# Subtracting the row maximum of the nine kept scores on GpSimd instead of VectorE, in a top-12 attention kernel

## The reference

```python
xn = layernorm(x)                                  # no scale, no shift
q, k, v = split_heads(xn @ Wqkv.T + bqkv)
q, k = layernorm(q) * gamma_q + beta_q, layernorm(k) * gamma_k + beta_k
aw = softmax(q @ k.T / sqrt(8))                    # 256 x 256 a head
kth = top_k(aw, 12)[-1]                            # the 12th largest of each row
aws = aw * (aw >= kth); aws /= aws.sum(-1) + 1e-8
o_s = aws @ v                                      # sparse part
o_l = softmax(q) @ (softmax(k).T @ v) / (z + 1e-6) # linear part
o = a * o_s + (1 - a) * o_l                        # a = sigmoid(alpha), one a head
y = x + o @ Wproj.T + bproj + (xn @ W[i] + b[i])   # i chosen once from the logits
```

## Time and profile before

| | before |
|---|---|
| median of 3 runs | 1330.32 us (1327.15 to 1330.66) |
| span of the profiled execution | 1331.1 us |
| VectorE busy | 95% of the span |
| ScalarE busy | 86% |
| GpSimd busy | 83% |
| TensorE busy (matmuls) | 78% |
| mean granted TensorE clock | 0.930 |

### The profile page before, as it was taken

One profiled execution on the slowest core, in us unless ns is written; L12 is line 12 of the kernel. 1 busy time (PEld: TensorE's weight loads), 2 busy tenths in 40 slices (PEclk: granted clock), 3 DMA queues, 4 the chain that ended last, 5 costly groups with the idle time before them and its releaser, 6 DMA issues.

```text
span 1331.1 us, 40027 instructions
## 1 busy us (share of the span) xinstructions
PE 1040.0 (78%) x8964; PEld 693.5 (52%) x8964; DVE 1260.1 (95%) x4916; ACT 1138.5 (86%) x3978; POOL 1110.9 (83%) x1458
## 2 busy tenths in 40 slices
PE   3787877778787878877888787777877788787776
PEld 1455555555455555555555455554555555555544
DVE  5799999999999999999999999999999999999995
ACT  3689998989899888989989899888989888898885
POOL 4588898979789888888879889798888888889874
PEclk9989999989899798998989989898998998989998
DMA  2222222112222122221112221112221212221210
GB/s 57 72 59 63 77 77 75 35 57 64 77 76 72 29 64 65 76 77 47 53 53 76 77 76 46 55 57 71 76 76 35 66 53 76 77 76 33 64 49 13
DMA packets 165131, 82.31 MB, mean 62 GB/s; under 512 B 7747, under 2 KB 164933, under 8 KB 164934
## 3 DMA queue, kind: packets, MB, share of 16 engines
q1 hardware_dynamic: 164934, 80.54, 20.9%
HBM read 42.77 MB, written 37.75 MB: 60 GB/s over the span
## 4 chain that ended last, share of the span: by engine, by line
DVE 57%; issue 33%; DVEq 6%; ACT 1%; POOL 1%; PE 1%; DMA 0%; SPq 0%; POOLq 0%
DVE rest L525 21%; DVE top L518 21%; DVE next L531 8%; DVEq L72 5%; DVE drop L615 2%; DVE o_sparse L574 1%; ACT e L719 1%; DVE den L566 1%; DVE k_sum L593 1%; DVE stats L582 0%; PE work_ps L910 0%; PE work_ps L911 0%; DVE x_mv L588 0%; DVE d_max L557 0%; DVE den L571 0%
## 5 line engine op out<-in xcount | busy, mean ns | idle before, releaser
L386 POOL TENSOR_SCALAR below<-e,next 128x256 bf16<-128x256 f32 x768 | 696.1, 922 | 21.5 <-DVE next L531 21.3
L719 ACT ACTIVATE e<-score_ps,drop 128x256 f32<-128x256 f32 x1024 | 472.4, 480 | 108.2 <-DVE drop L615 105.5
L838 PE MATMUL turn_ps<-ident,e 128*128 128x128 f32 x2048 | 429.9, 303 | 10.9 <-ACT kept L685 10.4
L525 DVE MATCH_REPLACE8 rest<-e 128x256 f32<-128x256 f32 x1024 | 413.3, 404 | 0.0
L531 DVE MAX8 next<-rest 128x8 f32<-128x256 f32 x1024 | 407.5, 408 | 0.0
L839 PE MATMUL turn_ps<-minus_huge,below 128*128 128x128 bf16 x2048 | 402.5, 232 | 0.0
L518 DVE MAX8 top<-score_ps 128x8 f32<-128x256 f32 x1024 | 359.4, 410 | 41.8 <-issue 21.7
L838 PEld LDWEIGHTS turn_ps<-ident,e 128*128 128x128 f32 x2048 | 312.2, 152 | 80.9 <-ACT kept L685 17.9
L685 ACT ACTIVATE kept<-turn_ps 128x512 f32<-128x512 f32 x512 | 285.1, 620 | 33.8 <-PE turn_ps L839 14.3
L839 PEld LDWEIGHTS turn_ps<-minus_huge,below 128*128 128x128 bf16 x2048 | 234.5, 115 | 0.0
L719 ACT ACTIVATION_READ_ACCUMULATOR e<-score_ps,drop 128x1 f32 x1024 | 217.1, 212 | 0.0
(11 more groups left out here) (141 smaller groups left out, 1540.6 us busy)
## 6 DMA issues: line engine op xcount, KB each, us to landing
part_slots<-part SPq DMA_DIRECT2D x128, 192.0 KB, 2.3
q_slots<-part_slots SPq DMA_DIRECT2D x64, 256.0 KB, 3.4
k_slots<-part_slots SPq DMA_DIRECT2D x64, 256.0 KB, 4.1
part_slots<-part SPq DMA_DIRECT2D x64, 128.0 KB, 1.9
x_sb<-in_L_attn_x SPq DMA_DIRECT2D x32, 128.0 KB, 3.6
x_res<-in_L_attn_x SPq DMA_DIRECT2D x32, 128.0 KB, 3.7
out_y<-out_sb SPq DMA_DIRECT2D x32, 128.0 KB, 4.2
w_ops<-in_L_ffn_W SPq DMA_DIRECT2D x1, 512.0 KB
```

What stands on the lines that cost most here:

```text
L386: nc.gpsimd.tensor_scalar(below[:, r, t, :], e[:, r, t, :], next8[:, r, t, TOPK - 9:TOPK - 8], None, ALU.is_lt).then_inc(s["below_pool"], 1)
L525: nc.vector.match_replace(rest[:, t, :], e8[:, (u_ - 1) % 2, t, :], e[:, (u_ - 1) % RING, t, :], REMOVED).then_inc(s["rest_ready"], 1)
L719: nc.scalar.activation(e[:, u_ % RING, t, :], score_ps[:, u_ % 2, t // 2, t % 2, :], ACT.Exp, bias=drop[:, u_ % 2, t, 0:1], accum_out=z[:, ...
L838: mm(dst, e[:, r, t, keys], ident[:], start=True, stop=False, is_transpose=True)
```

## The change

The subtraction leaves VectorE's slot. GpSimd does it, in each slot of an existing batch, behind its three comparisons and ahead of the work that followed those. It waits for the four searches of the unit (`top_ready`), and for the e8 of two units before (`e8_ready`), whose buffer it overwrites. VectorE now waits, before the first search of a unit, until the subtraction of two units before has read that buffer of `top` (`drop_ready`). A wait at GpSimd's set-up makes sure that the zeroes of `top` are written.

```diff
@@ gpsimd, set-up
             nc.gpsimd.memset(eps_row[:, :, D:VA], Z_EPS).then_inc(s["pool_const"], 1)
+            pool.wait_ge(s["pool_const"], 7)
@@ gpsimd, body, behind the three comparisons of a slot
+                    if exists(it):
+
+                        q = u_ % 2
+                        wait(pool, s["e8_ready"], g - 1)
+                        wait_alone(pool, s["top_ready"], TILES * (g + 1), s["waits_passed"])
+                        nc.gpsimd.tensor_tensor(drop[:, q], top[:, q], top[:, q, :, 1:2].to_broadcast(
+                            [P, TILES, 9]), ALU.subtract).then_inc(s["drop_ready"], 1)
                     if u_ == 1 and exists(it + 1):
                         normalise(it, 0)
@@ vector, body
                     if exists(it):
+                        wait(dve, s["drop_ready"], g - 1)
                         for t in range(TILES):
                             largest(g, q, t)
                     if before:
                         remove(u_, 0)
-                    if exists(it):
-
-                        dve.wait_ge(s["top_ready"], TILES * (g + 1))
-                        nc.vector.tensor_tensor(drop[:, q], top[:, q], top[:, q, :, 1:2].to_broadcast(
-                            [P, TILES, 9]), ALU.subtract).then_inc(s["drop_ready"], 1)
                     extra(u_, 0)
```

## The result

The changed kernel takes 1618.74 us (median of 4 runs, 1615.98 to 1619.83), the kernel before 1330.49 us in the same comparison: a ratio of 1.216, 95% interval [1.214, 1.219]. It is 288 us slower. The forecast was 1600, in a range of 1550 to 1665. The profiled execution has a span of 1614.0 us.

The account below looks back on a forecast made before the run. The prediction took a loop between GpSimd and ScalarE as the bound: 48.8 us a batch against 39.9, over 30 batches 267 us, plus 3 at the ends, on 1331.1 gives 1601, so 1600 us, range 1550 to 1665.

Parts of the forecast that it names:

- The loop: GpSimd and ScalarE hand work to and fro through eight links between successive units' exponentials, 48.8 us a batch, setting the pace.
- four GpSimd links: Stretches between exponentials of units 1-2, 3-4, 4-5 and 7-0, passing through GpSimd: 6.84, 8.62, 7.74 and 7.59 us.
- What VectorE saves is worth nothing: VectorE loses 256 subtractions, 61 us, and alone would take 38.0 us a batch, but the longer loop rules.
- The price on GpSimd: One 128x36 subtraction on GpSimd takes 0.26 us, 0.34 with the hand-over to the start of the exponential.
- The dear subtraction: Rival: the subtraction on GpSimd costs up to what a 512-column operation costs, up to 1721 us; chance 0.06.
- The last link: From unit 7's exponentials to the next unit 0's, through GpSimd's adds, comparisons and subtraction: 7.59 us.
- the hardware loop's turn: VectorE stands 2.7 us at each turn of the hardware loop; taken as covered, nothing added.
- The sum: Eight links make 48.8 us a batch against 39.9 before; 30 batches add 267 us, the ends 3.
- The rival of the clock: TensorE's clock drops and delays the last link by 2 us in each batch: 60 us more, 1660; chance 0.2.
- The rival that the slack holds: GpSimd runs ahead, drops come hardly late and VectorE stays the bound: faster, 1269 us, at the most 1248; chance 0.04.
- The long links are program order: Argument against slack: the long stretches between exponentials follow program order, which no engine may alter; first residue starts 4.46 us after unit 3's exponentials.
- The shared port: Two-input VectorE operations and GpSimd operations lock each other out; the median of 183 ns was taken against this beside comparisons.

Follow-up runs that it names:

- the doubled work: Changed kernel with each subtraction done twice on GpSimd, the first time into a spare tile: 1645.68 us, ratio 1.238 to the kernel before.
- the fastest: Changed kernel with only unit 4's subtraction (first in its slot) and unit 2's (ahead of the comparisons) on GpSimd, the rest on VectorE: 1302.07 us, ratio 0.979.
- unit 5 alone: Changed kernel with only unit 5's subtraction on GpSimd, behind its comparisons, the seven others on VectorE: 1443.13 us, ratio 1.084 to the kernel before.
- units 4 and 5 back: Changed kernel with the subtractions of units 4 and 5 returned to VectorE, the six others on GpSimd: 1507.27 us, ratio 1.133 to the kernel before.
- units 1, 3, 6 and 7: Changed kernel with only these units' subtractions on GpSimd, behind the comparisons, the others on VectorE: 1466.68 us, ratio 1.102 to the kernel before.
- all ahead of the comparisons: Changed kernel with all eight subtractions on GpSimd, but ahead of the slot's three comparisons: 1375.60 us, ratio 1.036 to the kernel before.

## Why the prediction was right, point by point

- **The loop.** Right, and link by link: seven of eight within 0.1 us. The runs with the doubled work show that it is this loop (only its four GpSimd links count), and the run with VectorE's work given back shows that VectorE is off it.
- **What VectorE saves is worth nothing.** Right: 256 subtractions put back cost nothing. Its size was wrong without harm: the busy time fell by 33.5 us, not 61. The subtractions' 81.6 us are gone, but VectorE's other instructions add up to 24 us more than before, and neighbours overlap by 24 us less. The pace of 38.0 us for VectorE alone was reached by no version (the fastest has 38.9, by d_max).
- **The price on GpSimd.** 0.26 forecast, 0.251 measured. The factor of two that the Trainium skill has for two-input work (GPSIMD Engine Reference, Engine selection) would give 0.37; here it is 251 against a median of 183 ns, 1.4 times. The dear subtraction as a rival is out.
- **The last link** was mis-sized: 7.59 forecast, 8.13 measured. The parts are taken apart above: the squares 0.24 later (0.18 of it the clock; 0.06 stay unexplained), the drop 0.20 later for VectorE's searches, 0.10 more at the hand-over. The second is the hardware loop's turn, which I had taken to be covered by ScalarE's slack: it is, but for some 0.2 us a batch. In the 25 batches the link is 7.69 to 8.80, in the one behind them 9.81.
- **The sum.** 49.2 for 48.8 us a batch (by d_max) makes 13 of the 19 us that were missing. Another 5.5 are the median of the runs, 4.7 above the profiled span, where I had taken it 0.8 below.
- **The rival of the clock.** The granted clock did fall, from 0.93 to 0.83 in the mean, and the q,k product is where it bites, as the rival said. Its 2 us came in one batch, where the product ran at the lower level throughout; in 10 others it was 0.43 in the mean. That is 6.3 us in all and not 60. The product at 0.50 took 4.51 for 2.48 us, 1.8 times and not twice.
- **The rival that the slack holds** was rightly put low. It was wrong in a way that I shared when I wrote what unit 5 alone would do: there is hardly any slack. One late link of 3.56 us made the batch 3.76 us longer. That a late drop also moves VectorE's small steps into collisions and waits is what the rows of that run suggest.
- **"The long links are program order"** was right for this kernel but too narrow as a rule. I named waits for ScalarE as what makes the drop late; the runs with units given back show GpSimd's backlog as a second cause, which takes over where the first is removed. That is what failed in the expectations for units 4 and 5 back and for units 1, 3, 6 and 7. For all ahead of the comparisons it is 1.8 of the 3.0 us, and the turn of the hardware loop the rest.
- **The shared port.** The prediction took the median of 183 ns to speak against a lock beside the comparisons. The trace shows such a wait in 31 of the 256 (last section): a median does not show what a few do.
- **What to look for.** d_max was to be 48 to 50 us apart: it is 47.9 to 51.0, all but two inside. Waits were to stand in units 2, 4, 5 and 0 and not in the others: so it is, but for four short ones. Squares that wait for TensorE were named as a sign of being wrong: GpSimd's adds wait for ScalarE, as forecast, but ScalarE's squares wait for TensorE in 11 of 29 batches, for 4.9 us in all.

## What to carry to other kernels

Before a small step is moved from the bounding engine to one that is free for 17% of the time, list what stands ahead of it in the new queue and what that work itself waits for, and add up the links from one consumer's start to the next: a step of 0.25 us can cost 9 us a batch by its place. Then see the queue as a whole: a place ahead of other work is free only where the queue would have stood still anyway, and what it pushes back has readers too. Move only those steps that are dear where they are (here the two of eight that collide) into gaps in which the other engine already waits.

## What the runs showed of the hardware that I had not expected

A subtraction on VectorE reads two tensors in SBUF. Where it starts well inside a two-input operation of GpSimd, it ends with that operation. Beside GpSimd's comparisons, which have one tensor input and a column of scalars, it waits only if it starts soon after one of them. VectorE's and GpSimd's order in time, from the run with unit 5 alone on GpSimd:

```profile
719.29 0.98 DVE L635 TENSOR_TENSOR drop<-top 128x36 f32<-128x36 f32 x1
...
744.60 0.19 DVE L635 TENSOR_TENSOR drop<-top 128x36 f32<-128x36 f32 x1
```

```profile
719.06 1.16 POOL L366 TENSOR_TENSOR residue<-qkT,part 128x512 f32<-128x512 f32 x1 [0.58 <-ACT part L723]
...
742.38 2.72 POOL L396 TENSOR_SCALAR below<-e,next 128x256 bf16<-128x256 f32 x3
```

The subtraction at 719.29 ends at 720.27, 0.05 us behind the residue (719.06 + 1.16 = 720.22); that at 744.60 takes 0.19 us in the midst of three comparisons (742.38 to 745.10). And from the kernel before, beside the comparisons that start at 688.85:

```profile
689.09 0.28 DVE L615 TENSOR_TENSOR drop<-top 128x36 f32<-128x36 f32 x1
```

It starts 0.24 us after a comparison and ends at 689.37, 0.52 us after that comparison's start and 0.40 us before its end. In the trace of the kernel before, 43 subtractions start well inside a two-input operation of GpSimd (0.1 us or more behind its start, 0.25 or more before its end); all end 0.05 to 0.06 us behind it. Beside comparisons there are 126. The 31 that start 0.08 to 0.26 us after the start of a comparison take 0.26 to 0.44 us, and all of them end 0.40 us before its end. The 82 that start later in it take 0.17 to 0.19 us, and so do 12 of the 13 that start within 0.05 us of a comparison's start.

The Trainium skill (SBUF — State Buffer, SBUF: two separate sides) has such a VectorE operation blocked by a GpSimd operation that reads SBUF, for the whole of it. The two-input operations agree. The comparisons differ, and the measurement decides: such a comparison, of 0.92 us, holds a subtraction back only until 0.52 us after its own start. Why it lets go there, and whether other one-input operations do the same, no run shows.
